# Merge blocks asked for first, weight parts at other prologue places, one tile's score in one piece, and the second half's broadcast gates on ScalarE's DMA queue

## What is computed

```python
def cross(ctx, q, mask, W, b):                 # q = layernorm(x)
    s = q @ ctx.T / sqrt(512); s = where(mask, -1e9, s)
    return softmax(s) @ ctx @ W.T + b
x = x + cross(ctx, layernorm(x), mask, W_merge, b_merge)
h = layernorm(x)
rw = gating(h)                                 # 16 weights for each row
q, k, v = (sum_e rw[e] * (h @ proj[e]) for proj in (q_proj, k_proj, v_proj))
a = softmax(causal(q @ k.T / 8)) @ v           # head width 64, over the batch's 512 rows
x = x + sum_e rw[e] * a @ o_proj[e]
...
```

## Time and profile before

| | |
|---|---|
| runs | 898.63, 899.1, 899.4 us; median 899.1 |
| the profiled execution, its own time | 897.96 us |
| its span, first to last instruction | 896.2 us |
| instructions | 15900 |
| TensorE busy | 871.1 us (97%) |
| VectorE busy | 637.3 us (71%) |
| ScalarE busy | 225.0 us (25%) |
| GpSimd busy | 127.2 us (14%) |
| granted TensorE clock, mean | 0.992 |

### The profile page before, as it was taken

How to read it: one execution, slowest core, us unless ns; L and a number is a source line. 1 busy time by engine, 2 the same in 40 slices (tenths; PEclk the granted TensorE clock), 3 DMA queues, 4 the chain that set the end, 5 groups by cost and what they waited for, 6 DMA issues and landing times.

```text
span 896.2 us, 15900 instructions
## 1 busy us (share of the span) xinstructions
PE 871.1 (97%) x4872; PEld 814.1 (91%) x4872; DVE 637.3 (71%) x1946; ACT 225.0 (25%) x567; POOL 127.2 (14%) x335
## 2 busy tenths in 40 slices
PE   6689999999999999999999999999999999999998
PEld 5689999999999999999999999999999999999996
DVE  6888868777586786767768577775767667576674
ACT  5522322213131222213212132221322112121131
POOL 5121111211011110111102011110111201011100
PEclk9799999999999999999999999999999999999999
DMA  9736415054141531425214351224415152131302
GB/s 320 288 121 167 151 51 142 27 154 129 49 132 39 164 107 61 120 59 176 84 62 120 99 166 53 86 84 130 150 38 148 35 136 92 35 98 36 97 25 94
DMA packets 68194, 96.96 MB, mean 108 GB/s; under 512 B 10905, under 2 KB 34105, under 8 KB 67874
## 3 DMA queue, kind: packets, MB, share of 16 engines
q1 hardware_dynamic: 59106, 86.79, 31.6%
q10 hardware_dynamic: 9024, 9.44, 4.5%
HBM read 77.07 MB, written 19.14 MB: 107 GB/s over the span
## 4 chain that ended last, share of the span: by engine, by line
issue 68%; PE 16%; POOLq 10%; POOL 3%; DMA 1%; DVE 1%; SPq 0%; DVEq 0%; ACT 0%; ACTq 0%
PE psQ L1328 9%; POOLq L616 2%; POOLq L596 2%; POOLq L619 2%; PE psM L1429 2%; PE psO L1429 2%; PE psQ L1429 1%; POOL limit L599 1%; POOLq L598 1%; POOLq L613 1%; POOLq L621 1%; POOL pow_out L622 1%; POOL pow_tmp L612 1%; DMA MASK<-in_mask 1%; DMA merge_lo<-merge_scratch 0%
## 5 line engine op out<-in xcount | busy, mean ns | idle before, releaser
L1328 PE MATMUL psQ<-Wqkv_hi,hT_hi 128*128 128x384 f32 (+1 forms) x1024 | 351.7, 343 | 1.8 <-DVE hT_lo L893 1.4
L1328 PE MATMUL psQ<-Wqkv_hi,hT_lo 128*128 128x384 f32 (+1 forms) x1024 | 347.3, 339 | 0.0
L1328 PE MATMUL psQ<-Wqkv_lo,hT_hi 128*128 128x384 f32 (+1 forms) x1024 | 347.2, 339 | 0.0
L1030 DVE SCALAR_TENSOR_TENSOR acc<-psQ,RW,acc 128x192 f32<-128x192 f32 x448 | 164.7, 411 | 116.5 <-PE psQ L1328 114.3
L1328 PEld LDWEIGHTS psQ<-Wqkv_hi,hT_hi 128*128 128x128 f32 x1024 | 193.7, 189 | 8.1 <-DVE hT_lo L893 1.8
L1328 PEld LDWEIGHTS psQ<-Wqkv_lo,hT_hi 128*128 128x128 f32 x1024 | 193.9, 189 | 4.6
L1328 PEld LDWEIGHTS psQ<-Wqkv_hi,hT_lo 128*128 128x128 f32 x1024 | 193.3, 189 | 0.0
L611 POOL TENSOR_TENSOR pow_tmp<-b_mv,eps 128x1 f32<-128x1 f32 x32 | 8.1, 254 | 670.5 <-DVE b_mv L983 670.5
L849 ACT ACTIVATE mixedT_hi<-spread 128x512 fp32r<-128x512 f32 x64 | 40.5, 632 | 189.2 <-DVE spread L1204 144.1
L1429 PE MATMUL psO<-Wo_hi,mixedT_hi 128*128 128x512 f32 x120 | 51.6, 430 | 0.2 <-DVE mixedT_lo L1192 0.2
L1429 PE MATMUL psO<-Wo_hi,mixedT_lo 128*128 128x512 f32 x120 | 47.2, 393 | 0.0
(11 more groups left out here) (206 smaller groups left out, 1305.3 us busy)
## 6 DMA issues: line engine op xcount, KB each, us to landing
X<-in_x SPq DMA_DIRECT2D x32, 256.0 KB, 2.7
x_scratch<-X SPq DMA_DIRECT2D x32, 256.0 KB, 2.0
spread<-gates_scratch ACTq DMA_DIRECT2D x16, 512.0 KB, 6.9
resid<-x_scratch SPq DMA_DIRECT2D x32, 256.0 KB, 4.4
out<-resid SPq DMA_DIRECT2D x32, 256.0 KB, 2.4
merge_hi<-merge_scratch SPq DMA_DIRECT2D x28, 256.0 KB, 2.9
merge_lo<-merge_scratch SPq DMA_DIRECT2D x28, 256.0 KB, 3.5
spread<-gates_scratch SPq DMA_DIRECT2D x14, 512.0 KB, 6.8
```

The source lines that it names most:

```text
L1030: dve.scalar_tensor_tensor(out=acc[e][:], in0=src, scalar=w, in1=acc[e][:], op0=ALU.mult, op1=ALU.add).then_inc(expert_added, 1)
L1328: last = pe.matmul(psQ[g % 4][:, 0:first_col(g) + PW], a[:, c * P:(c + 1) * P], w[:, c, E + g * PW - first_col(g):E + (g + 1) * PW], start ...
```

## The change

Five edits, all of them of order:

1. **SyncE.** `load_merge` at k = 17, 19, 21 and 23 stands ahead of the other transfers of its slot. At k = 19 these are the store of `X2`, the load of a context slice and of the context two batches ahead; at k = 21 the load of `X2`.
2. **SyncE and ScalarE.** The second half's broadcast (k = 3) goes from SyncE's list to ScalarE's, behind the exponential of k = 2 and ahead of the scaling of k = 4.
3. **Prologue of VectorE and ScalarE.** VectorE: the sigmoid of `gates` (3 small instructions) moves up in front of `low_ctx`, the scaling of `sim` down in front of `G_low`, `w_low(0)`'s first half in front of `add_x2`, its second half and `w_low(1)` around `normalise(0)`. ScalarE: `w_high(3)` and `w_high(4)` come before `copy_rows(0)`, and all eight parts are made before the first body, where before the last two stood in slots 0 and 1.
4. **GpSimd.** The root for `sim` moves behind the limits and the power of tile 3.
5. **Tile 5's score.** It is made from whole operands too (`WHOLE = 6`): 4 matmuls of 128x77 in place of 8 split ones, read from `XT[1]` directly, so `turned_high(5)` on ScalarE and `turned_low(5)` on VectorE go, and `x1_limit(5)` has 2 VectorE instructions in place of 4.

```diff
-W_AHEAD = 6
+WHOLE = 6
...
+        def is_whole(t1):
+            return isinstance(t1, int) and t1 < WHOLE
...
-                def load_spread(b, h):
...
+                        if qkv and k in G_AT:
+                            n = TILES * b + G_AT[k] + 1
+                            if live(n, N_TILES - TILES):
+                                load_merge(n, (G_AT[k] + 1) % TILES)
                         if prepare and g == SUM_SLOT + 1:
                             keep_x2(t + 1)
...
-                        if qkv and k in G_AT:
-                            n = TILES * b + G_AT[k] + 1
-                            if live(n, N_TILES - TILES):
-                                load_merge(n, (G_AT[k] + 1) % TILES)
-                        if lead and qkv and k == SPREAD_1_SLOT:
-                            load_spread(b - 1, 1)
...
-                    if n == 2:
+                    if n == TILES - 1:
                         pool.wait_ge(sim_floored, 1)
...
-                w_high(1)
-                w_high(2)
+                for g in range(1, 5):
+                    w_high(g)
                 copy_rows(0)
+                w_high(5)
+                w_high(6)
                 slice_high(1)
-                for g in range(3, W_AHEAD):
-                    w_high(g)
+                w_high(7)
...
-                        if qkv and is_first(b) and k + W_AHEAD < PAIRS:
-                            w_high(k + W_AHEAD)
...
+                        if lead and qkv and k == SPREAD_1_SLOT:
+                            load_spread(b - 1, 1)
...
-                        if cross and g == X1_HIGH_SLOT:
+                        if cross and g == X1_HIGH_SLOT and not is_whole(t1):
                             turned_high(t1, p1)
...
-                    if isinstance(t1, int) and t1 < X1_LEAD:
+                    if is_whole(t1):
                         dve.wait_ge(x1_scale_ready, t1 + 1)
...
+                dve.wait_ge(gate_e_made, 1)
+                link(dve.tensor_scalar(gate_e, gate_e, 1.0, None, ALU.add))
+                link(dve.reciprocal(gate_e, gate_e))
+                link(dve.tensor_scalar(neg_sig[:], gate_e, -1.0, None, ALU.mult))
+                low_ctx()
+                slice_low(0)
+                dve.wait_ge(ld_x[TILES], 32)
+                x1_moments(TILES, 0, x_first[TILES])
                 dve.wait_ge(sim_rooted, 1)
                 for c in range(KC):
                     last = dve.tensor_tensor(sim_f[:, c, :], sim_f[:, c, :], sim_rn, ALU.mult)
                 last.then_inc(sim_normed, 1)
-                low_ctx()
-                slice_low(0)
-                dve.wait_ge(ld_x[TILES], 32)
-                x1_moments(TILES, 0, x_first[TILES])
                 G_low(0)
+                w_low(0, 0)
                 x2_moved = add_x2(None)
                 row_stats(x2_moved)
-                w_low(0, 0)
                 dve.wait_ge(sim_hi, 1)
                 dve.tensor_tensor(simn[1], sim_f, simn[0].bitcast(F32), ALU.subtract).then_inc(sim_lo, 1)
+                w_low(0, 1)
                 normalise(0, 0)
-                w_low(0, 1)
+                w_low(1)
                 low_rows(0)
-                w_low(1)
-                dve.wait_ge(gate_e_made, 1)
...
                 w_low(2)
+                w_low(3)
                 slice_low(1)
-                w_low(3)
...
+                            if is_whole(t + X1_LEAD):
+                                x1_whole_score(t + X1_LEAD)
+                            else:
+                                x1_score(t + X1_LEAD, (j + 1) % 2)
```

More of the change, by code:

```diff
@@ L477, in store_gates @@
                     sp.dma_start(gate, gatesT[:]).then_inc(st_gates, 16)
-                def load_spread(b, h):
-                    gate = gates_dram[bass.ds(b, 1), h].rearrange("a e l -> (a e) l")
-                    half = 2 * b + h
-                    parts = [gate[part:part + E - 1:2, :].partition_broadcast(DH) for part in range(2)]
-                    if not is_first(b) or h:
-                        sp.wait_ge(mix_lo, 4 * half)
-                    sp.wait_ge(st_gates, 16 * half + 16)
-                    for part in range(2):
-                        sp.dma_start(spread[part * DH:(part + 1) * DH, :, :], parts[part]).then_inc(spread_in, 16)
                 def load_last_spread(u):
@@ L898, in turned_low @@
                 def turned_low(t1, p):
-                    dve.wait_ge(xt_hi, t1 - X1_LEAD + 1)
+                    dve.wait_ge(xt_hi, t1 - WHOLE + 1)
                     dve.tensor_tensor(hT[p][1][:], XT[p][:], hT[p][0][:].bitcast(F32), ALU.subtract).then_inc(xt_lo, 1)
@@ L1071, in _ @@
                 last.then_inc(sim_normed, 1)
-                low_ctx()
-                slice_low(0)
-                dve.wait_ge(ld_x[TILES], 32)
-                x1_moments(TILES, 0, x_first[TILES])
                 G_low(0)
+                w_low(0, 0)
                 x2_moved = add_x2(None)
                 row_stats(x2_moved)
-                w_low(0, 0)
                 dve.wait_ge(sim_hi, 1)
                 dve.tensor_tensor(simn[1], sim_f, simn[0].bitcast(F32), ALU.subtract).then_inc(sim_lo, 1)
+                w_low(0, 1)
                 normalise(0, 0)
-                w_low(0, 1)
+                w_low(1)
                 low_rows(0)
-                w_low(1)
-                dve.wait_ge(gate_e_made, 1)
-                link(dve.tensor_scalar(gate_e, gate_e, 1.0, None, ALU.add))
-                link(dve.reciprocal(gate_e, gate_e))
-                link(dve.tensor_scalar(neg_sig[:], gate_e, -1.0, None, ALU.mult))
                 w_low(2)
+                w_low(3)
                 slice_low(1)
-                w_low(3)
                 def body(b, qkv, lead):
@@ L1249, in x1_score @@
                 def x1_score(t1, p):
-                    bank = next_bank(xt_lo, t1 - X1_LEAD + 1, has_high=False)
+                    bank = next_bank(xt_lo, t1 - WHOLE + 1, has_high=False)
                     for c in range(KC):
@@ L1260, in x1_whole_score @@
                 def x1_whole_score(n):
-                    bank = next_bank(ld_xt[n], 16, has_high=False)
+                    if n < X1_LEAD:
+                        bank = next_bank(ld_xt[n], 16, has_high=False)
+                        tile = xt_first[n]
+                    else:
+                        bank = next_bank(xt_in, 16 * (n - X1_LEAD + 1), has_high=False)
+                        tile = XT[1][:]
                     if n == 0:
@@ L1267, in x1_whole_score @@
                     for c in range(KC):
-                        last = pe.matmul(bank[:, 0:C], xt_first[n][:, c * P:(c + 1) * P], ctx_f[n // TILES][:, c, 0:C],
+                        last = pe.matmul(bank[:, 0:C], tile[:, c * P:(c + 1) * P], ctx_f[n // TILES][:, c, 0:C],
                                          start=(c == 0), stop=(c == KC - 1))
@@ L1344, in body @@
                         if cross and g == X1_SCORE_SLOT:
-                            x1_score(t + X1_LEAD, (j + 1) % 2)
+                            if is_whole(t + X1_LEAD):
+                                x1_whole_score(t + X1_LEAD)
+                            else:
+                                x1_score(t + X1_LEAD, (j + 1) % 2)
                         if prepare and g == H_T_SLOT:
```

## The result

The changed kernel takes 893.11 us (median of 6 runs, 892.65 to 893.73), the kernel before 898.98 beside it (6 runs, 898.07 to 899.4). The ratio is 0.9938, interval 0.9926 to 0.995: 5.6 us faster by the ratio (4.5 to 6.7), where 4.2 were forecast. The profiled execution took 893.18 us, against 897.96 before: 4.8 us less.

What follows compares the result with a forecast made beforehand. TensorE, busy 97% of the span, was taken as the bound, so reordering only fills its waits. Terms -3.0 (H), +1.4 (clock) and -2.6 (merge) sum to -4.2 us, from 899.1 to 894.9 us; range 892.8 to 897.3.

Steps and rivals of the forecast that it cites:

- Rival A: First tile: the clock does not fall, or falls under the wait for H; 893.5 us, chance 0.20.
- The term for `H`, -3.0: First tile: VectorE and GpSimd's chain each move 2.97 us sooner, so H starts at 52.65 instead of 55.63; -3.0 us.
- I price the prologue at 0: Prologue: hT_lo should not move and the first body starts as before; 0 us, other end a loss of 1.4.
- A gain is excluded: Prologue: no earlier start is possible, since ScalarE's copy for tile 0 waits for TensorE's transposes.
- The limit: First tile: x1_limit(5) waits for GpSimd's 6.1 us chain, wait growing from 0.46 to about 1.0; saved instructions worth nothing.
- The clock, +1.4: First tile: a 2.2 us wait for H lowers TensorE's clock on work behind it; +1.4 us, ends 0 and 1.7.
- The merge term, -2.6: Merge products: earlier issue removes or shortens the merge_lo waits except batch 0's, 2.9 less 0.3; -2.6 us.
- Broadcast, 0: SyncE to ScalarE: the two issues, 1.34 us, fit into ScalarE's 2.30 us wait; worth 0 both ways.
- Rival E: ScalarE: broadcast issues block its list and delay k = 4's scaling; slower, 905.4 us at 7 us of blocking, chance 0.05.
- The whole score: First tile: dropping turned_low(5) saves VectorE 0.60 us of the 2.97; the one-piece score's 0.1 more on TensorE is hidden.

Runs made afterwards that it cites:

- e1: Kernel before with only the merge blocks asked for first on SyncE: 894.56 us, ratio 0.9966.
- e2: Kernel before with only the second half's broadcast issued from ScalarE's queue: 898.67 us, ratio 1.0005.
- e3: Kernel before with only tile 5's score made from whole operands: 899.17 us, ratio 1.001.
- e5: Changed kernel plus 14 matmuls with unused results ahead of tile 1's transposes, in the wait for H: 891.23 us, ratio 0.9917.
- e7: Changed kernel with tile 1's normalisation at the head of slot 4 on VectorE: 892.27 us, ratio 0.9926.
- e11: e8 plus tile 1's turned rows copied ahead of tile 5's exponential on ScalarE, and hT_lo made at the head of slot 5: 889.02 us, ratio 0.9896.
- e12: e11 plus e9's move of slice_low(1) into slot 0: 888.37 us, ratio 0.9886.
- e9: Changed kernel with VectorE's slice_low(1) moved from ahead of the first body to behind w_low(4) in slot 0: 892.14 us, ratio 0.9935.
- e6: Changed kernel with GpSimd making tile 5's limit ahead of tile 1's powers in the first body: 890.36 us, ratio 0.9907.
- e8: Changed kernel with both moves of e6 and e7, limit first and normalisation first: 889.37 us, ratio 0.9896.
- e4: Kernel before with only the prologue order on VectorE, ScalarE and GpSimd changed (edits 3 and 4): 896.36 us, ratio 0.9984.
- e10: Changed kernel with edit 5 undone, tile 5's score from split operands again: 892.65 us, ratio 0.9939.

## Why the prediction was right, and where it was off

The forecast was 894.9 us by three terms; the time is 893.1, within the range. The three terms were the right ones, each with its mechanism, but their sizes were off and made up for each other in part. By the number alone Rival A (893.5, no fall of the clock) is nearer; the profiled execution shows the fall, so that is chance. Step by step:

**The term for `H`, -3.0.** `H` starts 55.63 - 52.84 = 2.79 us earlier, but by another sum. The step "I price the prologue at 0" didn't see it: the first body starts 0.62 earlier. Of this, 0.23 stand already in the first transposes of the profiled executions (5.21 against 5.44), ahead of all that was changed. From those transposes to the first body the four executions with the old order (before, e1, e2, e3) take 25.71 to 25.93 us. Six with the new order take 25.32 to 25.83, 0.3 less on average. But the other four with the new order (e5, e7, e11, e12) have a longer half-speed spell in the prologue and take 26.31 to 26.97, so that over all ten the new order starts no earlier (25.9 against 25.8). "A gain is excluded" was thus too strong, since I looked only at the copy's wait in the earlier trace rows, but a gain isn't shown either. Inside the tile 2.18 came out in place of 2.97, since the context slice was 0.67 us late, a wait that the working didn't have. e9 shows it was on the path. The slice isn't late by the new order alone: e1 and e2 pay for it as well, and the execution behind the earlier trace rows happened to have it early.

**The limit.** That the instructions saved in `x1_limit(5)` go into a longer wait for GpSimd's limit was right (0.96 against 1.0), and so was the 6.1 us chain. e6, e7 and e8 show the rest: the limit first gains 2.8 us by the ratios, the normalisation first 1.1 at most, both 3.8, of which the clock has a large part. The Trainium skill's section on GpSimd's shared SBUF interfaces (GPSIMD Engine Reference, section 1, Specifications) stood behind keeping that chain long; the trace agrees, 1.61 us again beside `w_low(7)`. No run took the vector instruction away from beside it, but the traces show one of another length: in the prologue, beside the half part, the same GpSimd instruction took 0.95 us (before 0.81). Each time it ended 0.05 us behind the `w_low` beside it, 47.67 against 47.62 at tile 1 and 26.36 against 26.31 in the prologue.

**The clock, +1.4.** The fall was forecast, and the wait is 3.13 us where 2.2 was forecast, as TensorE arrived at 50.4 and not 51.1: it started 0.6 earlier. The spell of 3.41 us lies wholly on work, 1.7 us. As a term it is an average: of the six profiled executions with 2.6 to 3.1 us of waiting for `H`, it came in three (the changed kernel, e3, e9) and not in the other three (e2, e4, e10). The traces give its price: from the transposes on, the executions without merge waits above 0.2 us and without a spell there take 835.6 or 835.7 us (e1, e5, e6, e10), the changed kernel 837.9. Of these 2.3 us 1.7 are half of the 3.41 us at half speed; its merge wait of 0.34 is in the rest. The times say less. The mean clock of a run falls by 0.002 for 3.4 us at half speed. In e9 and e10, six runs each of nearly the same kernel, the three runs at 0.994 took 890.9 us on average, the four at 0.992 took 892.0, and the five at 0.989 or 0.990 took 893.6: 1.1 and 1.6 us a step. But the changed kernel's own six show no step, 893.1 at 0.992 (two) and 893.2 at 0.990 (four). In the kernel before, 30 of 31 runs gave 897.7, 898.2 and 898.8 for 0.994, 0.992 and 0.990: 0.5 to 0.6 a step, perhaps since there most of the spell lies under the wait for `H`. (The mean doesn't tell which spell it was.) Rival A, no fall, is thus no rival but another part of the executions. Where the long wait is shorter or gone the fall is rarer or gone too: in the 23 runs of e5, e6, e8, e11 and e12 no mean clock is under 0.992.

**The merge term, -2.6.** All waits that were to go went, and only batch 0's stayed (in e1, e5 and e11 it is gone too, in the others it is 0.2 to 0.3). The size was wrong. I took the idle time in the rows, and by the cut e1 gained 4.3 us for rows of 2.9. In batch 1 it can be read directly. From the start of the turned probabilities to the third product it was 203.80 - 202.62 = 1.18 us, after the change

```profile
201.22 0.27 PE L1333 MATMUL psT<-ident,probs 128*128 128x128 f32 x1
201.24 0.48 PE L1271 MATMUL psO<-merge_hi,att_hi 128*78 128x512 f32 x1
201.56 0.40 PE L1271 MATMUL psO<-merge_lo,att_hi 128*78 128x512 f32 x1
201.79 0.39 PE L1271 MATMUL psO<-merge_hi,att_lo 128*78 128x512 f32 x1
```

it is 0.57: 0.61 us for a wait shown as 0.42. With batch 0's wait left, the term is about -3.7. This is the step that was most off, 1.1 us.

**Broadcast, 0.** Right, e2. Rival E stays far: ScalarE's scaling is still released by VectorE, with 2.30 us of cover in e2 and 2.29 in the changed kernel.

**The whole score.** The prediction gave it 0.60 us as part of the first term. In company that holds (0.6 in the traces, e10 and e4 against e9); alone it gained 0.5 us in the tile, and the time was 0.9 us longer by the ratio, e3. The kernel's time doesn't show it either way, 0.9938 with it and 0.9939 without.

**The sum.** Forecast 0, -3.0, +1.4, -2.6. Measured in the profiled executions -0.6 (start), -2.2 (tile), +1.7 (clock), -3.7 (merge): -4.8. (The last is what is left of the 2.0 behind the transposes once the spell is taken out, so it isn't a measurement of its own; e1's 4.3, less what batch 0's wait costs, agrees with it.) Against the medians it is 5.9, since the profiled execution before lay 1.0 us under the median of its six runs and the one after on its own; the forecast had carried that over. The four single edits give 4.0, -0.1, -0.6 and 2.2 us by their medians, 5.4 together. By their ratios they give 3.1, -0.4, -0.9 and 1.4, 3.1 together, where the whole gives 5.6. Each of these has 0.8 to 1.2 us of uncertainty to either side, so it isn't shown whether the parts add up to the whole.

**What stays open.** Why the clock falls behind a wait of 3.1 us in one execution and not in the next; and why the prologue's spell is 13.65 us in the profiled executions of e5, e7, e11 and e12 and 10.24 in the other ten. The edits of these four against the changed kernel lie at the prologue's end or behind it, but all four have the new prologue order, and none of the four executions with the old order has the long spell. Chance and the new order are both possible, and nothing was run that tells them apart. The 0.7 us of e11 hang on it.

## What to carry to other kernels

When an engine is the bound and its waits follow each other, cut the trace at the points where it is released, and compare stretch by stretch: an edit that shortens the first wait lengthens the next one, until the last release itself is earlier. Look for the clock in each stretch: a half-speed spell that lies under a wait is free, and an edit that removes an earlier wait can put it on work, so that an edit that is right alone measures as a loss. Where a long wait can't be removed, reorder what feeds it: here two GpSimd instructions and one normalisation put ahead of others gave 3.8 us more than the change's own 5.6, by the traces some 1.5 of it from the shorter path and 1.7 because the clock no longer fell. Before a stretch is compared with another execution's, look whether a transfer came late in one of them: the context slice alone moved the first tile of the same program by 0.3 and 0.8 us.

## What the runs showed of the hardware

A short wait of TensorE for a landing costs about 0.2 us more than its idle time in the row (0.61 for 0.42; 4.3 for 2.9 over seven; by the same cut 4.0 for 2.3 over five in e2 and 3.9 for 2.7 over six in e4). What the rows show of it is that the matmul behind the wait doesn't overlap with the one ahead, where without a wait it starts 0.02 us behind the transpose's start. Its weights, too, are loaded only behind the landing. Before, ahead of the matmul at 203.31, and after the change, ahead of the one at 201.24:

```profile
203.28 0.14 PEld L1274 LDWEIGHTS psO<-merge_hi,att_hi 128*78 128x78 f32 x1 [0.70 <-issue]
```

```profile
201.22 0.15 PEld L1271 LDWEIGHTS psO<-merge_hi,att_hi 128*78 128x78 f32 x1
```

Waits of the same length, in the same place, were followed by different clocks: 3.12 (e3) and 3.13 us (the changed kernel) by a granted 0.50, 3.06 (e10), 3.07 (e4) and 3.09 us (e2) by 1.00. In the kernel before and in e1, 1.74 and 1.75 us were followed by a fall, and 1.75 us in e2 were not. So no length of wait seen here decides it.

A GpSimd instruction on 128x1 that started 0.05 to 0.2 us behind a `w_low` of VectorE (a subtraction of two 128x768 or 128x1536 tiles) ended 0.05 us behind it: it took 1.61 us beside a `w_low` of 1.72 us and 0.81 and 0.95 beside halves of 0.92 and 0.95 us. With none beside it, it took 0.19.
